# Transposing DMAs in place of matrix-engine transposes in a four-block layer kernel

## The reference

```python
x = x + tanh(g_xattn[0]) * L0_xattn(layernorm(x), ctx, Wq, Wkv, Wout)      # 8 heads, rope, softmax over 128
x = x + tanh(g_ffn[0])   * L0_ffn(layernorm(x), fast_b, w_fc, w_proj, u, v, gate)
x = x + tanh(g_xattn[1]) * L1_xattn(layernorm(x), ctx, W, b)               # x @ W1.T + mean(ctx) @ W2.T + b
x = x + tanh(g_ffn[1])   * L1_ffn(layernorm(x), w1, b1, w2, b2)

# L0_ffn
scale = clip(mean(abs(w), axis=1), 1e-05)
w = clip(round(w / scale), -1, 1) * scale
h = x @ w_fc.T + gate * (x @ v.T @ fast_b.T @ u.T)
return (relu(h) ** 2) @ w_proj.T
# L1_ffn: both matmuls with one scale for a whole weight, activations rounded to 127 steps of a row's
# largest value after an rmsnorm, gelu between them
```

## Time and profile before

| | us |
|---|---|
| median of three runs | 1386.57 (1384.86 to 1387.01) |
| the profiled execution, its own time | 1387.25 |
| its span, first to last instruction | 1385.4 |
| PE busy | 1239.8 (89%) |
| DVE busy | 1010.7 (73%) |
| ACT busy | 854.7 (62%) |
| POOL busy | 526.4 (38%) |
| DMA queue of SP, its packets' share of 16 engines | 18.0% |

### The profile page before, as it was taken

One profiled execution on the slowest core, in us unless ns is written; L12 is line 12 of the kernel. 1 busy time (PEld: TensorE's weight loads), 2 busy tenths in 40 slices (PEclk: granted clock), 3 DMA queues, 4 the chain that ended last, 5 costly groups with the idle time before them and its releaser, 6 DMA issues.

```text
span 1385.4 us, 24630 instructions
## 1 busy us (share of the span) xinstructions
PE 1239.8 (89%) x8500; PEld 815.9 (59%) x8788; DVE 1010.7 (73%) x2102; ACT 854.7 (62%) x1613; POOL 526.4 (38%) x484
## 2 busy tenths in 40 slices
PE   5634757899999999999999999999999999999875
PEld 3423544766666666757575757575767666665532
DVE  2688647787777778786968786868787877776654
ACT  1274654575858585757576676767585758485534
POOL 1134469533425151616152524333433434251320
PEclk9655878999999999999999999999999999999987
DMA  8245633202010111111120202020202020100000
GB/s 300 92 171 174 236 106 119 58 1 73 17 63 24 61 27 61 27 48 28 53 69 16 72 15 72 15 72 15 72 3 81 4 69 18 46 17 31 0 16 16
DMA packets 51565, 85.06 MB, mean 61 GB/s; under 512 B 5424, under 2 KB 23344, under 8 KB 49840
## 3 DMA queue, kind: packets, MB, share of 16 engines
q1 hardware_dynamic: 49216, 82.07, 18.0%
q10 hardware_dynamic: 2304, 2.40, 0.5%
HBM read 57.97 MB, written 9.18 MB: 48 GB/s over the span
## 4 chain that ended last, share of the span: by engine, by line
issue 34%; DVE 22%; ACT 18%; POOL 12%; PE 11%; DMA 2%; POOLq 0%; SPq 0%; DVEq 0%; ACTq 0%
ACT e L710 7%; DVE h L1230 4%; POOL rs L497 3%; POOL hid L506 3%; ACT rl L742 2%; POOL r L518 2%; PE ps L1580 2%; ACT h L771 2%; ACT q L775 2%; POOL e L501 2%; ACT sq L753 2%; PE ps L1503 1%; PE ps L1490 1%; DVE qS L1080 1%; DVE r L940 1%
## 5 line engine op out<-in xcount | busy, mean ns | idle before, releaser
L497 POOL TENSOR_TENSOR rs<-ve,nhalf 128x1 f32<-128x1 f32 x160 | 96.0, 600 | 594.1 <-DVE ve L1072 425.4
L1490 PE MATMUL ps<-xT,fcT 128*128 128x256 f16 x2048 | 260.9, 275 | 0.0
L1503 PE MATMUL ps<-pjT,hid 128*128 128x512 fp8e4 x1024 | 242.2, 386 | 2.2 <-POOL hid L506 2.2
L1490 PEld LDWEIGHTS ps<-xT,fcT 128*128 128x128 fp8e4 x2048 | 202.3, 99 | 26.6
L506 POOL TENSOR_TENSOR hid<-sq,hid 128x512 f16<-128x512 f32 x128 | 157.3, 1234 | 21.6 <-ACT sq L753 14.4
L1503 PEld LDWEIGHTS ps<-pjT,hid 128*128 128x128 f16 x1024 | 96.4, 99 | 98.0 <-issue 6.1
L742 ACT ACTIVATE rl<-ps,rsf 128x256 f32<-128x256 f32 x256 | 107.8, 478 | 43.7 <-PE ps L1490 43.7
L710 ACT ACTIVATE e<-ps,nmb,sig 128x128 f32<-128x128 f32 x256 | 113.4, 463 | 23.8 <-DVE nmb L1116 23.8
L1580 PE MATMUL ps<-w2T,hT 128*128 128x512 fp8e4 x512 | 118.6, 386 | 5.8 <-ACT hT L787 5.8
L780 ACT ACTIVATE q<-h 128x2048 f16<-128x2048 f32 x32 | 61.1, 1911 | 96.6 <-DVE h L1241 96.6
L1555 PE MATMUL ps<-w1T,q4T 128*128 128x512 fp8e4 x512 | 119.2, 382 | 0.0
(11 more groups left out here) (209 smaller groups left out, 2431.5 us busy)
## 6 DMA issues: line engine op xcount, KB each, us to landing
h<-in_w SPq DMA_DIRECT2D x12, 1024.0 KB, 5.1
xb<-in_x SPq DMA_DIRECT2D x16, 512.0 KB, 3.4
qS<-qT SPq DMA_DIRECT2D x128, 64.0 KB, 2.0
r1b<-r SPq DMA_DIRECT2D x16, 512.0 KB, 3.0
out<-r SPq DMA_DIRECT2D x32, 256.0 KB, 2.5
xa<-in_x SPq DMA_DIRECT2D x15, 512.0 KB, 3.6
rope<-in_rope SPq DMA_DIRECT2D x16, 384.0 KB, 3.2
hid<-in_w SPq DMA_DIRECT2D x4, 1024.0 KB, 6.2
```

The costliest lines, as they stand in the source:

```text
L497: pool.tensor_tensor(rs[:, n, t:t + 1], ve[:, n, t:t + 1], nhalf[:, :], ALU.pow).then_inc(done, 1)
L1490: mm = pe.matmul(dst, fcT[:, k, f * P:(f + 1) * P], xT2[:, xs, k, :], start=False, stop=(xs == 1 and k == KC - 1))
L1503: mm = pe.matmul(ps[:, FFN0 + t, :], hid[:, xs, c, t * P:(t + 1) * P], pjT[:, c, :], start=(c == 0 and xs == 0), stop=(c == FC - 1 and xs ...
```

## The change

All PE transposes of tokens and probabilities go. ACT rounds the token-major tile to 16 bits (`x16a`, `x16f`, `x16b`, `p16`), POOL (for x1, x2 and x3) or DVE (for the probabilities) makes the lo part beside it, and a transposing DMA on SP's queue writes the operand. `q4` and `q5` are turned the same way. A group has 14 transposing DMAs: ten of 128x1024 elements, two of 128x512 (q4), two of 128x2048 (q5), all of 2 bytes. That is 10 x 256 KB + 2 x 128 KB + 2 x 512 KB = 3840 KB, or 120 blocks of 128x128.

```diff
-            def t2(g, t):
-                if t == 1:
-                    need(pe, x1_done, TILES, g, 0)
-                need(pe, xn2_done, TILES, g, t)
-                for k in range(KC):
-                    mm = pe.transpose(att_bank(16 + t)[:, k * P:(k + 1) * P], xn2[:, t, k * P:(k + 1) * P], ident[:, :])
-                mm.then_inc(t2_ps, 1)
...
+            def x2_hi(g, t):
...
+                need_dma(act, xT2_in[t], g - 1)
+                need(act, xn2_done, TILES, g, t)
+                act.activation(x16f[:, t, 0, :], xn2[:, t, :], ACT.Copy).then_inc(x2hi, 1)
...
+            def x2_lo(g, t):
+                need(pool, x2hi, TILES, g, t)
+                rest(x16f[:, t, 1, :], xn2[:, t, :], x16f[:, t, 0, :], x2lo)
...
+            def turn_x2(g, t):
+                if t == 0:
+                    need(sp, up_ps, FC // 2, g - 1, FC // 2 - 1)
+                need(sp, x2lo, TILES, g, t)
+                sp.dma_start_transpose(xT2[:, :, :, t * P:(t + 1) * P].rearrange("p s k n -> p (s k) n"),
+                                       x16f[:, t, :, :].rearrange("p s n -> p (s n)")).then_inc(xT2_in[t], 16)
...
+            def turn_q5(g, t):
...
+                sp.dma_start_transpose(hT[:, t, :, :], q5[:, :]).then_inc(hT_in[t], 16)
```

The low-rank rows move to the bank of the up pieces, and `up` has its low-rank matmul last:

```diff
             def low_rows(g):
...
-                        mm = pe.matmul(att_bank(18)[:, 0:G], vrep[:, vs, k, :], xT2[:, xs, k, :],
+                        mm = pe.matmul(ps[:, FFN0 + 1, 0:G], vrep[:, vs, k, :], xT2[:, xs, k, :],
...
-                    pe.matmul(dst, lowA[:, f * P:(f + 1) * P], tlow[:, :], start=True, stop=False)
...
+                    if m == 0 and a == 0:
+                        need(pe, low_done, 1, g, 0)
+                    mm = pe.matmul(dst, lowA[:, f * P:(f + 1) * P], tlow[:, :], start=False, stop=True)
```

The second FFN's weights come transposed from the host and are rounded in place (DVE, ACT, DVE) with no signs, no PE and no POOL; the eight pieces of the first FFN keep the old way with both comparisons on DVE (`ON_POOL = ()`):

```diff
-        PLACE = [(1, 2, 3, 0)[n % 4] if n < 16 else 2 + n % 2 for n in range(len(LOADS))]
+        PLACE = (1, 4, 0, 2, 3, 1, 4, 0) + (2, 3, 1, 4, 0, 2, 3, 4) + (2, 3) * 4
...
+            def round_weights(n):
...
+                dve.tensor_scalar(src, src, winv1[:, w:w + 1], MAGIC, ALU.mult, ALU.add).then_inc(c_round, 1)
...
+                    act.activation(lifted[n % 2], piece[PLACE[W0 + n]], ACT.Relu, bias=lift[:, :]).then_inc(c_lift, 1)
...
+                dve.tensor_scalar(dst, lifted[n % 2], 2.0, 1.0, ALU.min, ALU.subtract, saturate=False)\
+                    .then_inc(c_clip, 1)
```

More of the change, by code:

```diff
@@ L247, in arrived @@
+        SUM0, W0 = 8, 16
         def arrived(eng, n):
             eng.wait_ge(d_piece[PLACE[n]], 16 * PLACE[:n + 1].count(PLACE[n]))
[L251 to L266, removed]
@@ L296, in due, with used @@
[L296 to L303, removed]
+        def used(eng, n):
+            if n < SUM0:
+                eng.wait_ge(c_quant, n + 1)
+            elif n < W0:
+                eng.wait_ge(c_asum, n - SUM0 + 1)
+            else:
+                eng.wait_ge(c_lift, n - W0 + 1)
@@ new lines, in build, with moments @@
+        placed = {}
+        for eng, tables in AT.items():
+            for name, places in tables.items():
+                for g in range(GROUPS):
+                    own = OWN[eng].get(g)
+                    for k, p in enumerate(own[name] if own else places):
+                        placed.setdefault((eng, name, p if own else p + g * SLOTS), []).append((k, g))
+        def moments(eng):
+            return sorted({p for e, _, p in placed if e == eng} | {p for places in PREP[eng].values() for p in places})
@@ L305, in sign_parts, with due, here @@
+        def due(eng, name, p):
+            return placed.get((eng, name, p), ())
+        def here(eng, name, p):
+            return [k for k, at in enumerate(PREP[eng][name]) if at == p]
         def sign_parts(q):
@@ L310, in sign_parts @@
                         for c in range(KC)]
[L311 to L314, removed]
+            return [(0, PIECE, thr[:, FC + i:FC + i + 1], nthr[:, FC + i:FC + i + 1])]
         def first(g):
[L317 to L333, removed]
+            return g == 0
         block = ctx.enter_context(nc.Block())
@@ L479, in _ @@
+            run()
             for t in range(TILES):
@@ L565, in prepare, with run @@
+                for _ in here("POOL", "bound", p):
                     largest(c_bnd, 4, c_bndmax, bmaxa[:, :], bmax[:, :])
-                for _ in here(POOL_PREP["wx"], p):
+                for _ in here("POOL", "wx_max", p):
                     largest(c_wmax, 4, c_wmaxa, wmaxa[:, 3:4], wmax[:, 3:4])
-            def body(j):
-                for s in range(SLOTS):
-                    for m, g in due(POOL_AT["hid"], j, s):
+            def run():
+                for p in moments("POOL"):
+                    for m, g in due("POOL", "hid", p):
@@ L1012, in prepare @@
                     weight_max(2, d_small, 128, vT_sb.rearrange("p k r -> p (k r)"))
-                for _ in here(DVE_PREP["wo_scale"], p):
+                for _ in here("DVE", "wo_scale", p):
                     weight_scale(1, 1, 3)
@@ L1345, in prepare @@
                     mm.then_inc(c_lowps, 1)
-                for _ in here(PE_PREP["mix"], p):
+                for _ in here("PE", "mix", p):
                     pe.wait_ge(d_wc, 16)
```

1243 lines of the change are left out of this document (669 added, 574 removed).

## The result

The changed kernel takes 1351.72 us (median of four runs, 1341.82 to 1352.64; two more gave 1345.93 and 1350.05) against 1386.38: a ratio of **0.9732, 95% interval 0.9695 to 0.9768**. I had forecast 1283 and a range of 1245 to 1345. The sign was right, and a third of the saving came (34.7 of 103 us).

The account below looks back on a forecast made before the run. PE was taken to set the pace in the middle, chains through several engines at both ends. From 1387.2 us, 79 came off for 14 periods (72.45 to 66.8), 29 off the start, 4 onto the end: 1283, range 1245 to 1345.

Parts of the forecast that it names:

- The transposes, 7.5 us a group off: Steady period on PE: removing transposes and most waits before them takes 7.5 us off 72.5, leaving 65.0.
- A wait of 1.1 us: PE, each group: `up` follows `low_rows` at once and waits 1.1 us for `tlow`, covered only by eight matmuls.
- The clock, which I held at 1.00: PE's granted clock in the middle: full at 1.00; a lower one was listed as making the prediction wrong.
- to 35 us a group: POOL's load, with six more subtractions, rises from 27.8 to 35 us a group, not near 65.
- x2's DMA, 0.9 us: PE before `low_rows`: x2's chain takes 12.0 us against 11.2 of cover, so 0.9 us of waiting a group.
- the heads' DMA: Heads' re-pairing: three `up` pairs (5.9 us) cover what took 6.0, so 0.1 us a group is added.
- The start: Up to group 0's first `up` unchanged at 156.9 us; from there to group 1's 71 us, 29 saved.
- The end: After group 15's first `up`: 7.5 us of transposes saved, 11.5 added by three DMAs and subtractions; 4 us lost.
- The first (the queue fills): SP's queue or the DMA engines become the bound, priced per 128x128 block: 1505 us, chance 0.11.
- The second: Transposing DMAs land in 6 us or more, queue not full; period near 70, 1334 us, chance 0.17.
- The third: The start doesn't shorten: DVE takes all comparisons and 100 us remain; 1312 us, chance 0.10.
- the fourth: No stalls at all, low and x2 covered: period 65.2, start 66 us, 1255 us, chance 0.17.

Follow-up runs that it names:

- tlow_short: Changed kernel, groups 3 to 13: ACT copies `tlow` ahead of rounding x1's second tile, DVE makes its parts ahead of normalising that tile; 1330.72 us.
- filler: Changed kernel with ten matmuls of unused result put into PE's wait for `tlow`, groups 3 to 13; 1336.75 us.
- hid_earlier: Changed kernel with POOL's last two subtractions of `hid` moved ahead of norm 2 and norm 3, groups 3 to 13; 1341.01 us.

## Why the prediction was wrong, by its own steps

**The transposes, 7.5 us a group off: held.** From 583.08 to 655.28 PE's waits are 2.32 + 1.95 + 0.50 us and the slow clock about 1.7, so 72.2 - 6.5 = 65.7 us are work and small gaps, against the 65.0 that I had.

**"A wait of 1.1 us" for `tlow`: mis-sized, 2.32 measured.** The place and the mechanism were right. I took the chain's length from the trace before (1.95 us behind `low_rows`). In the changed order ACT's rounding of x1's second tile stood ahead of the copy, and a cast of DVE (0.61 us in place of 0.28) ran beside POOL's subtraction. tlow_short took both away and measured 1.14. Share of the miss: 1.2 us a group.

**The clock, which I held at 1.00: this step failed.** I had named it as what would make the prediction wrong "because PE now waits often", and gave it neither a price nor a chance. filler put the price at 1.4 to 1.7 us a group, more than my whole term for the wait. In the changed kernel's trace it is paid nine times in eight periods.

**POOL "to 35 us a group" and "None of them nears 65": the step that failed for `hid`.** It answers for POOL's load, which was right (36.27 us in one period). It says nothing of the order, and the 1.95 us of wait came from four operations in front of two. hid_earlier showed that this is not a free 1.95: behind it stand the probabilities, which take it back.

**x2's DMA, 0.9 us: no wait at all** in the middle. The other terms: wo's wait for `qS` 0.5, where I had nothing, and none for the heads' DMA, where I had 0.1. Together 1.2 + 1.7 + 1.95 + 0.5 - 0.9 - 0.1, with 0.7 more of work and 0.3 that I had rounded away, is 5.4 us, the 72.2 less 66.8.

**The start: held** (153.4 and 72.1 against 156.9 and 71). **The end: failed, to the good**, 107 against 120. I had added 11.5 us for three DMAs and subtractions and not taken off what they replaced: in the trace before, the first of the two last `w2_down` stood behind 16 identity matmuls (1.89 us) and a wait of 4.03 us for ACT's copies out of PSUM. A wait for the DMA stands there now, in their place and not on top:

```profile
1318.67 5.31 PE L1693 MATMUL ps<-w2T,hT 128*128 128x512 fp8e4 x16 [2.68 <-DMA hT<-q]
1330.38 6.29 PE L1693 MATMUL ps<-w2T,hT 128*128 128x512 fp8e4 x16 [6.40 <-DMA hT<-q]
```

That is not all of it. Before, the last two tiles' `w1_up` were one run (1348.72 to 1357.05 us), and ACT's last rounding for q5 ended 15.3 us behind it, at 1372.31. Now the first tile's ends at 1303.60 and the second's at 1315.99, and ACT's last rounding ends 9.8 us behind that, at 1325.81. The two tiles seem to queue less at ACT and DVE, which I had not looked at. This is read from the rows and was not tried.

**The rivals.** The first (the queue fills) is out: SP is at 26 of 72 us, and even with twice as many (24 x 1.25 + 4 x 1.31 + 7.9 = 43 us) the kernel takes 0.9875 of the time before. The second is out as well: landing is 3.1 us. The third is out, as the start did shorten, and so is the fourth, as PE does wait. The time came nearest to the second rival's 1334, for a reason that none of them had. By the row of the landing, the Trainium skill's 1309 ns a block ("VectorE: DVE Perf Modes", "The three transpose paths") does not add up over the blocks of a DMA: eight land in 3.1 us. The Trainium skill's other rule ("Advanced Engine Details and Errata", "X-Bar Transpose (TRN2)"), that transposing DMAs are as fast as regular ones, is nearly right for 256 KB, 3.1 against 2.9 us, and not for 512 KB, 4.3 against 2.9.

## What to carry to other kernels

When a change takes work off the engine that was full, that engine starts to wait, so price each chain that it now meets by the order of the programs around it, not by the load of the engines. Price the clock too: behind a wait of about 2 us on PE a slow clock can cost 1.6 us more, and shortening the wait for `tlow` by half gave back both there. A wait that is removed uncovers the next one, 2.0 us for 1.95 at `p_v` and wo; follow that chain before counting a gain.

## What was not expected of the hardware

- The granted clock fell behind idle stretches of 1.95 to 2.3 us in some groups and not in others of the same kernel: behind 2.32 us at `tlow` (hid_earlier, both ways), and behind 1.95 us at `hid` (the changed kernel, at 485.07 but not at 631.18). It did not fall behind the 1.14 us at `tlow` in any group of tlow_short. Which stretches are hit isn't settled.
- DVE's cast of 32x256 takes 0.28 us, and 1.17 beside a subtraction of POOL that started 0.13 us earlier.
- A transposing DMA takes SP 1.24 us whether it has four blocks or eight, and 1.77 with sixteen; a plain one takes 0.6.
